# A fused attention and gated-FFN block on one core: the head of the kernel is reordered (loads of x, statistics, first products)

## The reference

```python
def reference(x, Wq, bq, Wk, bk, Wv, bv, ln_w, gate_w, up_w, down_w):   # x: 1 x 2048 x 512
    xn = layernorm(x)
    q = einsum('bse,edh->bsdh', xn, Wq) + bq          # 16 x 32 per token
    k = repeat(einsum('bse,edh->bsdh', xn, Wk) + bk, 4, axis=-1)    # 16 x 8, repeated
    v = repeat(einsum('bse,edh->bsdh', xn, Wv) + bv, 4, axis=-1)
    attn = softmax(einsum('bsdh,bseh->bsde', q, k) / 4)    # 16 x 16, within each token
    s = einsum('bsde,bseh->bsdh', attn, v).reshape(..., 512)
    nx = xn * rsqrt(mean(xn**2) + 1e-5) * ln_w
    g = silu(nx @ gate_w.T) * (nx @ up_w.T)           # 1792 wide
    return x + s * silu(g @ down_w.T)
```

## Time and profile before

| | |
|---|---|
| time, median of 3 runs | 475.04 us (474.88 to 475.17) |
| the profiled execution | 474.35 us, its span 472.6 us |
| granted TensorE clock, mean | 1.000 |
| PE busy | 466.3 us (99%), 2122 matmuls |
| DVE busy | 412.7 us (87%) |
| ACT busy | 244.2 us (52%) |
| POOL busy | 123.1 us (26%) |

### The profile page before, as it was taken

The page is one execution under the profiler, slowest core; times in us unless marked ns, Lnnn a source line. Parts: engine busy times, 40 slices in busy tenths (PEclk is TensorE's granted clock), DMA queues, the critical chain, the costliest instruction groups (busy, mean ns, idle before and its releaser), DMA issues.

```text
span 472.6 us, 6217 instructions
## 1 busy us (share of the span) xinstructions
PE 466.3 (99%) x2122; PEld 391.0 (83%) x2122; DVE 412.7 (87%) x561; ACT 244.2 (52%) x417; POOL 123.1 (26%) x106
## 2 busy tenths in 40 slices
PE   7999999999999999999999999999999999999997
PEld 7898888888888888888888888888888888888886
DVE  6889778987898898889989898999998888888994
ACT  4785656658588888654122545225225335358102
POOL 5740312126222122233443101000011111126920
PEclk9999999999999999999999999999999999999999
DMA  8605996579779996573474649546556655514772
GB/s 269 252 2 225 345 380 262 234 259 273 205 248 301 298 360 255 188 268 133 135 235 162 218 187 371 202 184 223 222 201 223 223 200 200 201 44 135 276 259 89
DMA packets 44623, 105.70 MB, mean 224 GB/s; under 512 B 20272, under 2 KB 21808, under 8 KB 41264
## 3 DMA queue, kind: packets, MB, share of 16 engines
q1 hardware_dynamic: 44592, 105.31, 63.3%
HBM read 69.90 MB, written 35.40 MB: 223 GB/s over the span
## 4 chain that ended last, share of the span: by engine, by line
PE 95%; DVE 2%; DMA 1%; ACT 1%; SPq 0%; POOL 0%; issue 0%
PE gu_ps L553 18%; PE gu_ps L555 18%; PE gu_ps L556 18%; PE y_ps L687 8%; PE y_ps L688 8%; PE y_ps L689 8%; PE gu_ps L688 3%; PE gu_ps L687 3%; PE gu_ps L689 3%; PE gu_ps L718 2%; PE gu_ps L715 2%; PE gu_ps L714 2%; DMA xz<-x 1%; DVE w_ops L1166 1%; PE y_ps L727 0%; DVE stats L1075 0%
## 5 line engine op out<-in xcount | busy, mean ns | idle before, releaser
L553 PE MATMUL gu_ps<-z_hi,w_ops 128*128 128x512 f32 x378 | 147.2, 390 | 0.1
L556 PE MATMUL gu_ps<-z_hi,w_ops 128*128 128x512 f32 x378 | 147.1, 389 | 0.0
L555 PE MATMUL gu_ps<-z_lo,w_ops 128*128 128x512 f32 x378 | 147.1, 389 | 0.0
L498 POOL TENSOR_TENSOR h_lo<-h,h_hi 128x512 fp32r<-128x512 f32 x28 | 37.4, 1335 | 226.8 <-ACT h_hi L916 226.6
L553 PEld LDWEIGHTS gu_ps<-z_hi,w_ops 128*128 128x128 f32 x378 | 71.0, 188 | 15.5 <-issue 0.4
L556 PEld LDWEIGHTS gu_ps<-z_hi,w_ops 128*128 128x128 f32 x378 | 70.9, 188 | 14.8
L555 PEld LDWEIGHTS gu_ps<-z_lo,w_ops 128*128 128x128 f32 x378 | 70.9, 188 | 14.5
L687 PE MATMUL y_ps<-wd_ops,h_hi 128*128 128x512 f32 x168 | 65.6, 390 | 0.0
L689 PE MATMUL y_ps<-wd_ops,h_lo 128*128 128x512 f32 x168 | 65.5, 390 | 0.0
L688 PE MATMUL y_ps<-wd_ops,h_hi 128*128 128x512 f32 x168 | 65.5, 390 | 0.0
L916 ACT ACTIVATE h_hi<-h 128x512 fp32r<-128x512 f32 x28 | 17.6, 630 | 58.9 <-DVE h L1208 58.9
(11 more groups left out here) (139 smaller groups left out, 753.0 us busy)
## 6 DMA issues: line engine op xcount, KB each, us to landing
w_kept<-w_ops SPq DMA_DIRECT2D x13, 1792.0 KB, 6.2
w_ops<-w_kept SPq DMA_DIRECT2D x13, 1792.0 KB, 7.6
wd_ops<-wd_kept SPq DMA_DIRECT2D x35, 512.0 KB, 4.0
raw<-gate_up SPq DMA_DIRECT2D x30, 256.0 KB, 3.9
wd_kept<-wd_ops SPq DMA_DIRECT2D x14, 512.0 KB, 7.8
xz<-x SPq DMA_DIRECT2D x16, 256.0 KB, 5.3
raw<-down SPq DMA_DIRECT2D x14, 256.0 KB, 8.5
w_ops<-wd_kept SPq DMA_DIRECT2D x7, 512.0 KB, 7.5
```

The costliest lines, as they stand in the source:

```text
L498: pool.tensor_tensor(lo, src, hi.bitcast(F32), ALU.subtract).then_inc(h_lo_done, 1)
L553: pe.matmul(acc, w_h, z_hi[:, zi, c, :], start=start and c == 0, stop=False, skip_group_check=True)
L555: pe.matmul(acc, w_h, z_lo[:, zi, c, :], start=False, stop=False, skip_group_check=True)
L556: end = pe.matmul(acc, w_l, z_hi[:, zi, c, :], start=False, stop=c == 1, skip_group_check=True)
```

## The change

- SP loads tiles 0 and 2 of x; ACT's own queue loads tiles 1 and 3 and `lnw`, ahead of the table load. SP then loads gate and up of group 0, `wk`, `wv`, the halves of `wq`, tiles 4 to 6, the biases, tile 7.
- Statistics in twos: two `stats_tile`, two `aggregate`, one tensor_scalar for both variances, one root of two columns on POOL.
- POOL normalises tile 0; DVE tiles 1 to 3.
- POOL runs `rms_of(0, J, 1, 0)` behind `scale_tile(J)` instead of ahead of `sum_queries(0)`.
- DVE's order behind the normalisation is `z_lo_tile(0)`, `x_variance(0)`, `z_lo_tile(1)`, `first_lo(0)`, `z_lo_tile(2)`, `(3)`, `first_lo(1)`. ACT runs `first_hi(1)` ahead of `z_raw_tile(0)`, and `hi_qkv(1)` behind `z_raw_tile(2)`.
- PE warms up with 24 transposes, and `first_products` forms the gate product in two halves of the block's tokens where it waits for them.
- `qkv_product` waits for the halves of its weights one by one.

```diff
-    WARM_UP = 32
+    WARM_UP = 24
...
-            load_x(0, range(0, J))
-            sp.dma_start(lnw_sb[:], lnw).then_inc(lnw_in, 16)
+            load_x(0, (0, 2))
             load_gate(0)
+            load_up(0)
+            sp.dma_start(wqkv_raw[:, :, DG:2 * DG], wk.rearrange("(k p) n -> p k n", p=P)).then_inc(wkv_in, 16)
+            sp.dma_start(wqkv_raw[:, :, 2 * DG:], wv.rearrange("(k p) n -> p k n", p=P)).then_inc(wkv_in, 16)
             for a in (0, 2):
                 sp.dma_start(wq_raw[:, a:a + 2, :], wq.rearrange("(k p) n -> p k n", p=P)[:, a:a + 2, :])\
                   .then_inc(wq_in[a // 2], 16)
-            load_up(0)
...
-            load_x(0, (J,))
+            load_x(0, range(J, JJ - 1))
...
-            load_x(0, range(J + 1, JJ))
+            load_x(0, (JJ - 1,))
...
+            def scale_two(j):
+                pool.wait_ge(var_done, j + 2)
+                t = slice(j, j + 2)
+                pool.tensor_tensor(z_scale[:, t], z_var[:, t], minus_half[:, t], ALU.pow).then_inc(z_scale_done, 2)
+
+            def normalise_first():
+                pool.wait_ge(z_scale_done, 2)
+                pool.tensor_scalar(xz[:, 0, :], xz[:, 0, :], mean_var[:, 0, 0:1], z_scale[:, 0:1],
+                                   ALU.subtract, ALU.mult).then_inc(z_pool_done, 1)
...
-            for j in range(J):
-                scale_tile(j)
-            pool.wait_ge(var_done, J + 1)
-            rms_of(0, J, 1, 0)
+            scale_two(0)
+            normalise_first()
+            scale_two(2)
             sum_queries(0)
             sum_queries(1)
             scale_tile(J)
+            pool.wait_ge(var_done, J + 1)
+            rms_of(0, J, 1, 0)
             pool.wait_ge(bias_in, 48)
...
+            def first_products():
+
+                gate, up = gu_ps[:, GATE_BANK, :], gu_ps[:, UP_BANK, :]
+                gates = [(wi, zi, c) for wi, zi in ((WA11, ZB11), (WA12, ZB21)) for c in range(2)]
+                ups = [(wi, zi, c) for wi, zi in ((WA21, ZB11), (WA22, ZB21)) for c in range(2)]
+                halves = slice(0, TB // 2), slice(TB // 2, TB)
...
                 pe.wait_ge(w_hi_a, 1)
+                for a, t in enumerate(halves):
+                    pe.wait_ge(z_hi_done, 2 * a + 2)
+                    for n, (wi, zi, c) in enumerate(gates):
+                        pe.matmul(gate[:, t], w_part(0, wi, c), z_hi[:, zi, c, t], start=a + n == 0, stop=False,
+                                  skip_group_check=True)
+                pe.wait_ge(z_lo_done, 2)
+                for wi, zi, c in gates:
+                    pe.matmul(gate[:, halves[0]], w_part(0, wi, c), z_lo[:, zi, c, halves[0]], start=False, stop=False,
+                              skip_group_check=True)
                 pe.wait_ge(w_lo_a, 1)
+                for wi, zi, c in gates:
+                    pe.matmul(gate, w_part(1, wi, c), z_hi[:, zi, c, :], start=False, stop=False, skip_group_check=True)
+                pe.wait_ge(w_hi_a, 2)
+                for n, (wi, zi, c) in enumerate(ups):
+                    pe.matmul(up, w_part(0, wi, c), z_hi[:, zi, c, :], start=n == 0, stop=False)
                 pe.wait_ge(z_lo_done, J)
+                for n, (wi, zi, c) in enumerate(gates):
+                    end = pe.matmul(gate[:, halves[1]], w_part(0, wi, c), z_lo[:, zi, c, halves[1]], start=False,
+                                    stop=n == 3, skip_group_check=True)
                 end.then_inc(m2_done, 1)
...
+            for j in (1, 3):
+                act.dma_start(xz[:, j, :], x_tiles[j]).then_inc(x_in[j], 16)
+            act.dma_start(lnw_sb[:], lnw).then_inc(lnw_in, 16)
             load_silu()
...
+            first_hi(1)
             z_raw_tile(0)
             z_raw_tile(1)
-            first_hi(1)
             hi_qkv(0)
+            z_raw_tile(2)
             hi_qkv(1)
-            z_raw_tile(2)
             z_raw_tile(3)
...
-            for j in range(J):
+            for j in (0, 2):
                 stats_tile(j)
-                if j:
-                    variance(j - 1)
-                if j > 1:
-                    normalise_tile(j - 2)
-            variance(J - 1)
-            normalise_tile(J - 2)
+                stats_tile(j + 1)
+                aggregate(j)
+                aggregate(j + 1)
+                two_variances(j)
+            for j in range(1, J):
+                normalise_tile(j)
+            z_lo_tile(0)
             x_variance(0)
-            normalise_tile(J - 1)
+            z_lo_tile(1)
             first_lo(0)
-            for j in range(J):
-                z_lo_tile(j)
+            z_lo_tile(2)
+            z_lo_tile(3)
             first_lo(1)
```

More of the change, by code:

```diff
@@ L575, in eight, with w_part @@
                 return end
-            def first_gate0():
-                acc = gu_ps[:, GATE_BANK, :]
-                chunks = [(wi, zi, c) for wi, zi in ((WA11, ZB11), (WA12, ZB21)) for c in range(2)]
-                pe.wait_ge(w_hi_a, 1)
-                pe.wait_ge(z_hi_done, J)
-                for n, (wi, zi, c) in enumerate(chunks):
-                    pe.matmul(acc, w_ops[:, 0, 0, wi, c * P:(c + 1) * P], z_hi[:, zi, c, :], start=n == 0, stop=False)
-                pe.wait_ge(w_lo_a, 1)
-                for wi, zi, c in chunks:
-                    pe.matmul(acc, w_ops[:, 0, 1, wi, c * P:(c + 1) * P], z_hi[:, zi, c, :], start=False, stop=False)
+            def first_products():
[3 more added lines that the diff above has]
+                halves = slice(0, TB // 2), slice(TB // 2, TB)
+                def w_part(s, wi, c):
+                    return w_ops[:, 0, s, wi, c * P:(c + 1) * P]
+                pe.wait_ge(w_hi_a, 1)
+                for a, t in enumerate(halves):
[7 more added lines that the diff above has]
+                              skip_group_check=True)
+                pe.wait_ge(w_lo_a, 1)
+                for wi, zi, c in gates:
[3 more added lines that the diff above has]
+                    pe.matmul(up, w_part(0, wi, c), z_hi[:, zi, c, :], start=n == 0, stop=False)
@@ L591, in first_gate0 @@
                 end.then_inc(m2_done, 1)
[L593 to L599, removed]
-                    pe.matmul(acc, w_h, z_lo[:, zi, c, :], start=False, stop=False)
+                for wi, zi, c in ups:
+                    pe.matmul(up, w_part(0, wi, c), z_lo[:, zi, c, :], start=False, stop=False)
@@ L601, in first_up0 @@
                 pe.wait_ge(w_lo_a, 2)
-                for n, (wi, zi, c) in enumerate(chunks):
-                    end = pe.matmul(acc, w_ops[:, 0, 1, wi, c * P:(c + 1) * P], z_hi[:, zi, c, :], start=False,
-                                    stop=n == 3)
+                for n, (wi, zi, c) in enumerate(ups):
+                    end = pe.matmul(up, w_part(1, wi, c), z_hi[:, zi, c, :], start=False, stop=n == 3)
                 end.then_inc(m4_done, 1)
@@ L723, in transpose_tile @@
                     pe.wait_ge(z_act_done, j - J + 1)
+                elif j == 0:
+                    pe.wait_ge(z_pool_done, 1)
                 else:
-                    pe.wait_ge(z_done, j + 1)
+                    pe.wait_ge(z_done, j)
                 for k in range(K):
@@ L1056, in _, with aggregate, two_variances, variance @@
         def _(dve):
-            def variance(j):
+            def aggregate(j):
                 dve.wait_ge(bn_done, j + 1)
                 dve.bn_aggr(mean_var[:, j, :], stats[:, j, :]).then_inc(stats_done, 1)
+            def two_variances(j):
+                dve.wait_ge(stats_done, j + 2)
+                dve.tensor_scalar(z_var[:, j:j + 2], mean_var[:, j:j + 2, 1], 1.0 + EPS, EPS * EPS,
+                                  ALU.mult, ALU.add).then_inc(var_done, 2)
+            def variance(j):
                 dve.wait_ge(stats_done, j + 1)
```

27 lines of the change are left out of this document (11 added, 16 removed).

## The result

| | before | after |
|---|---|---|
| time, median | 474.96 us (474.88 to 475.17, 4 runs) | 478.03 us (477.96 to 478.26, 4 runs) |
| ratio to before, 95% interval | | 1.0068 (1.0056 to 1.0080) |
| profiled execution, its span | 474.35, 472.6 | 478.26, 476.4 |
| first steady product on PE | 41.74 | 45.49 |

The changed kernel is slower by 3.07 us on the medians. The forecast was +1.7, 476.7, with a range up to 478.2: the sign is right, the time lies at the upper end of the range, and the size is nearly half short.

A forecast was written before the change was run, and what follows sets the result against it. TensorE was taken to bound the kernel, its end moving with S. Q = 14.95 gave S = 22.1 against 20.36, so +1.7 us on the median 475.04: 476.7, range 474.9 to 478.2.

The forecast's parts named there:

- What sets the end: TensorE from qkv_product(2) on: its start follows S by 2.53 us, so the kernel's end moves by the change of S.
- S: Start of z_tile(5) on ScalarE, which waits for GpSimd's shift: forecast 22.1, against 20.36 before.
- Q: Start of stats_tile(4) on VectorE: forecast 14.95 with collisions, 13.95 without, against 15.53 before.
- S from Q: GpSimd's queue behind stats_tile(4): rms_of adds 2.3 us at its new place, giving S = Q + 7.13.
- The loads, statistics and roots: Front of the kernel: first two tiles land near 3.8, two-column root takes 0.71, the pair's 1.90 leads to 5.7.
- GpSimd's normalisation: Tile 0 normalised on GpSimd, ahead of the second pair's root: 1.03 us taken, bounds 0.6 and 1.8.
- n: Start of the last normalise_tile on VectorE: forecast 8.9, bounds 8.35 and 9.9, against 9.00 before.
- Collisions: VectorE's first_lo taking turns with GpSimd's sum_queries, both with two SBUF inputs: 1.0 us added, bounds 0 and 1.7.
- Rival 1: The forecast itself: GpSimd's later roots, with collisions, cost +1.0 to +2.6 us, time 476.7; chance 0.55.
- Rival 2: GpSimd's later roots without collisions, its normalisation short: +0.2 to +0.9 us, time 475.6; chance 0.25.
- Rival 3: Faster: the earlier first product reaches the end, needing Q below 13.2 or S not ruled by GpSimd: 473.5; chance 0.12.
- Rival 4: TensorE's clock falls to 1.2 GHz in a hole behind the warm-up: +2.3 us beyond the forecast, 479; chance 0.08.

The follow-up runs named there:

- e7: The changed kernel with rms_of back ahead of sum_queries and VectorE normalising all four tiles: 475.40 us, ratio to before 1.0010.
- f1: The kernel before with tile 5's statistics ahead of lo_qkv, its root ahead of the bias sums, two qkv `_lo` parts behind tile 4's transposes: 474.74 us, ratio 0.9994.
- f2: The changed kernel with f1's order, VectorE normalising all tiles, wq loaded earlier, z_lo_tile ahead of first_lo, 36 warm-up transposes and other reorderings: 474.82 us, ratio 0.9996.
- f3: f2 with the query sums held until the four normalisations, statistics of tiles 4 to 6 ahead of lo_qkv, tile 6's root earlier, transposes reordered: 473.83 us, ratio 0.9971.
- e2: The kernel before with only rms_of(0, J, 1, 0) moved behind scale_tile(J): 478.25 us, ratio to before 1.0078.
- e4: The changed kernel with 40 warm-up transposes instead of 24: 477.84 us, ratio to before 1.0069.
- e3: The changed kernel with VectorE normalising all four tiles, tile 0 included: 477.11 us, ratio to before 1.0056.
- e5: The changed kernel with GpSimd's sum_queries held back until both first_lo of VectorE are done: 478.25 us, ratio to before 1.0068.
- e1: The changed kernel with rms_of(0, J, 1, 0) back ahead of sum_queries on GpSimd: 476.34 us, ratio to before 1.0038.

## Why the prediction was right in sign and short in size

**What sets the end: right for a later S, and only for that.** In before, after and the seven experiments up to e7 the span less S lies between 452.0 and 452.3, while S itself goes from 20.36 to 24.80. But "whatever PE did before" and "the end of the kernel moves by the change of S" hold one way only: in the kernel before TensorE's own stream ended together with the chain through S, and in f1, f2 and f3 an S nearer to Q or earlier did not bring the end with it. The forecast did not meet this, since S moved later.

**S from Q: right.** The forecast was Q + 7.13; measured are 7.02 in after, 7.03 in e2 and e4, 7.02 in e3 (in e5 the gated sums set S instead). rms_of on a train of GpSimd without slack costs 2.2, for which 2.3 were taken. e1 takes it back.

**The loads, statistics and roots: right, a little short.** The pair's statistics start at 4.06 (3.8 taken, just outside the bound of 4.0). The root of two columns takes 0.71, as interpolated. Together they put the first root at 6.02 instead of 5.7. The second pair was there in time, as taken.

**GpSimd's normalisation: the first term that was mis-sized.** 2.08 us, for which 1.03 was taken, with 1.8 as the upper bound. The nearest rows were two-tensor additions, and one tensor in was held to be no dearer. In all four profiles that have it (after, e1, e4, e5) it took 2.08; VectorE does the same tile in 0.53. In all four VectorE's normalisation of tile 1 ran inside it, so how much of the 2.08 is the meeting and how much the instruction is not separated. Since the second pair's root stands behind it on GpSimd, n came at 10.1 instead of 8.9, of which about 1.0 is this term, outside the bounds given for n (8.35 to 9.9). The Trainium skill (GPSIMD Engine Reference, section 3.1) gives 769 ns for 512 elements as the best case; the measured 2.08 us is 2.7 times that, and here the measurement decides. The Trainium skill's statement that VectorE is about twice as fast for elementwise work (GPSIMD Engine Reference, section 8) points the right way and is too mild for these rows: 2.08 to 0.53 is nearly four times.

**Collisions: the second term.** 1.0 was added and 2.2 came. I had carried over the 0.85 that a train of four lost in the kernel before as the price of a collision. But that train had started late in the sums: it met their last two instructions (13.18 to 14.93), and two of its four went free. In after each of the four met one. Rows of VectorE and GpSimd from all engines in order of time, near 13 us and near 14 us of after:

```profile
12.56 0.81 DVE L1197 SCALAR_TENSOR_TENSOR w_ops<-raw,lnw_sb,w_ops 128x128 fp32r<-128x128 f32 x1
12.57 0.66 POOL L522 TENSOR_TENSOR qkv<-h_kept 128x256 f32<-128x256 f32 x1
...
13.18 1.09 POOL L519 TENSOR_TENSOR h_kept<-h_kept 128x512 f32<-128x512 f32 x1
13.29 1.12 DVE L1197 SCALAR_TENSOR_TENSOR w_ops<-raw,lnw_sb,w_ops 128x128 fp32r<-128x128 f32 x1
```

GpSimd's four instructions of the sums end at 12.49, 13.23, 14.27 and 15.00, VectorE's four at 12.64, 13.37, 14.41 and 15.15. They take turns, one for one: each of VectorE's ends 0.14 to 0.15 behind one of GpSimd's, and a train of four that starts with the sums takes about as long as they do. The bound should have been the whole length of the sums (some 3.5 us) less 1.1, that is 2.4, instead of 1.7. How many of the four meet one hangs on when wq lands: the sums were taken to start near 10.6 and started at 11.44 in after. In e4 they did start at 10.58, and n to Q was 6.5 instead of 7.2, so, by that run, some 0.7 of the 2.2 us are that landing.

**The sum of it.** S moved by 3.98 where 1.7 was forecast. n gives +1.2 of the difference, n to Q +1.2 (collisions), Q to S -0.1: together 2.3, which is the difference.

**From S to the time.** On S the change is +3.98 and on the profiled executions +3.9, but on the medians +3.07. The profiled execution of before (474.35) lies 0.6 below the median of its runs, and below all four (474.88 to 475.17); that of after (478.26) lies 0.2 above its own. Two other profiled kernels with the same single load queue, e2 and f1, have the third tile at 6.01 and 5.99, where the profile of before has it at 5.20, and n is 9.81 and 9.79 there; their profiled executions are slow ones of their runs (478.54 of 477.93 to 478.55, and 475.29 of 474.29 to 475.88). A later third tile in those four runs of before would account for the 0.6; that is inferred from those two, not seen in a run of before. With the experiments the kernel before also ran at 474.2 to 474.5. The prediction added its sum to the median as if the profiled execution were typical. Had the two terms been right, this habit would have made it 479, too high and outside the range. The mistakes partly cancelled, and that the measured time lies inside the range is in that part luck.

**PE.** "The first product near 8.8" was wrong: 11.47. GpSimd's instruction is only a part of that: in e3, without it, the first product still starts at 10.05, behind transposes from 8.04 and ScalarE's two rounded copies from 8.73, for which the 8.8 leaves no room. The waits at tiles 5 and 6 were 1.02 and 0.56, forecast 1.7 and 0.8, since PE came there later. The two halves of the first product were not tried alone; in e7, which has them, nothing of a gain is seen.

**The rivals.** Rival 1 happened: the later roots cost what was taken (2.2 for 2.3), GpSimd's normalisation and the collisions more. Rival 2 (no collisions, a short normalisation) failed on both: the normalisation took 2.08, and first_lo(0) met the sums; e5 shows that keeping them away by a wait costs the same at tile 4's root. Rival 3 was far: Q would have had to lie 4.1 us earlier than it did. Rival 4 happened in its first half: the clock did fall, to 0.50. Its second half, the 2.3 us, did not follow, as e4 shows: the slow products lay ahead of a wait for first_lo(0), not at the end of PE's chain.

## What to carry to other kernels

Before work is moved later on an engine, count what stands behind it at the new place: rms_of had 1.76 us of slack behind it at the old one and none at the new, and 2.2 us went to the end. Work at a place may also be a spacer: with rms_of gone, the sums ran into VectorE's instructions (e2), and every fix of one meeting made another (e1, e5) until the sums lay beside work that reads PSUM (f3). Cost a collision by what is left of the train on the other engine, not by one meeting. Ask for an earlier start as well as for a later one which chain comes next: here an S 0.8 us later cost its full length (e7, in the span), and an S 2.46 us earlier gave back 0.7 (f3). And take a saving at the front as real only when each later wait, one after the other, moves with it.

## What the runs showed of the hardware

- A GpSimd tensor_scalar of 128x512 float32 with two per-partition scalars took 2.08 us in each of the four profiles that had it. The query sums of the same size (tensor_tensor) took 1.03 to 1.11, and 1.23 once (f2); another tensor_tensor of that size took 1.82 (L504 in the earlier trace rows). Beside the 2.08 VectorE's own tensor_scalar kept its 0.53 (7.54 in after, inside 6.84 to 8.92).
- Beside GpSimd's additions VectorE's tensor_scalar did not: in f2 four normalisations, which have one tensor in, took 3.19 us instead of 2.14. The rule in the earlier trace rows was written for two tensors in and is too narrow. The Trainium skill has the wider form (GPSIMD Engine Reference, section 8, which counts VectorE instructions in a 2-port mode too, and VectorE: DVE Perf Modes, section "Mode 2×_2P", by which a float32 tensor_scalar from SBUF to SBUF runs in it); f2's rows agree. The 0.53 in after does not: there VectorE's tensor_scalar ran undisturbed beside GpSimd's own, and the measurement decides.
- Beside GpSimd's roots VectorE's train of two-input instructions kept its 1.13 (e1: from 11.88, the roots from 11.45 on), where beside the sums it took 3.15 to 3.40 (e3, after, e1, e7).
- The cost goes both ways: tile 4's root on GpSimd took 1.26 beside lo_qkv in before and after, and 0.55 in e5, between lo_qkv's two instructions, and in f3, ahead of them.
- Behind 24 warm-up transposes and a hole on PE the granted clock fell to 0.50 for some 3 us in after, e1, e5 (idle 2.08 to 2.13 us) and e7 (1.88), and stayed at 1.00 in e3 (1.71) and in e4 (40 transposes, 0.45). From e7 and e3, whose heads differ little, I can't say what decides it; that stays open.
